# Two fused transformer-like layers on one core: another order of TensorE's work in the attention loop, the routing fold moved into its first units, finer waits at GpSimd's gathers, and a shorter computation of the tile table

## The reference

```python
# x: 32 sequences x 64 tokens x 512 (2048 tokens)
# layer 0: h = x @ cond_w[subject];  x += (silu(h @ gate * gs) * (h @ up * us)) @ down * down_s
# layer 1, attention: 8 query heads, 4 key/value heads of 64; a paged cache of 16-token blocks
q, k = rope(rms(x Wq)), rope(rms(x Wk)); v = x Wv
k_blocks, v_blocks get the new tokens' rows; keys and values are read back through the block table
scores = q k^T / 16, allowed: key position in (pos - 256, pos]
y = softmax(scores) v @ Wo
# layer 1, mixture: logits = clip(y @ gate_w.T); top 2 of 8 experts; rw = softmax(top_w)
# each expert adds a sparse matrix (4096 entries) to W:
# x += y @ W.T + sum_k rw_k * sparse[top_k](y)
```

## Time and profile before

| | us |
|---|---|
| three timed runs | 984.15, 997.46, 1004.24 (median 997.46) |
| the profiled execution | 991.06 |
| its span, first to last instruction | 989.5 |
| TensorE busy | 888.9 (90% of the span) |
| VectorE busy | 651.2 (66%) |
| ScalarE busy | 382.9 (39%) |
| GpSimd busy | 431.0 (44%) |
| mean granted TensorE clock | 0.937 of full |

### The profile page before, as it was taken

How to read it: one execution, slowest core, us unless ns; L and a number is a source line. 1 busy time by engine, 2 the same in 40 slices (tenths; PEclk the granted TensorE clock), 3 DMA queues, 4 the chain that set the end, 5 groups by cost and what they waited for, 6 DMA issues and landing times.

```text
span 989.5 us, 15012 instructions
## 1 busy us (share of the span) xinstructions
PE 888.9 (90%) x4085; PEld 637.7 (64%) x4085; DVE 651.2 (66%) x1875; ACT 382.9 (39%) x869; POOL 431.0 (44%) x492
## 2 busy tenths in 40 slices
PE   5699998999899999967898999998999985999994
PEld 5688656874687478525566666665656654888773
DVE  5654589867886799495657767777766762444332
ACT  2522232224222332464545556766655530111110
POOL 3302334444344300005434665556565523666773
PEclk8599998999999999995879999999999996999998
DMA  8645454023302310544223344434333204743772
GB/s 230 239 127 197 159 198 138 1 49 81 92 1 46 120 43 1 173 147 118 77 60 93 76 115 104 113 104 128 102 97 90 61 23 130 223 148 87 126 114 31
DMA packets 66360, 105.44 MB, mean 107 GB/s; under 512 B 29811, under 2 KB 31107, under 8 KB 66158
## 3 DMA queue, kind: packets, MB, share of 16 engines
q0 software_dynamic: 30368, 50.69, 20.2%
q1 hardware_dynamic: 34974, 52.14, 17.0%
q10 hardware_dynamic: 944, 1.74, 0.6%
HBM read 91.63 MB, written 37.49 MB: 130 GB/s over the span
## 4 chain that ended last, share of the span: by engine, by line
PE 50%; DVE 16%; DMA 14%; issue 8%; POOL 4%; ACT 4%; SPq 2%; DVEq 0%; POOLq 0%; ACTq 0%
PE bank L799 14%; PE bank L810 8%; PE bank L948 6%; PE bank L933 6%; DMA mine<-list_dram 6%; PE bank L922 4%; PE bank L913 3%; PE bank L832 3%; DMA q_t<-q_dram 3%; POOL out_dram L2044 2%; DMA up_raw<-in_up_t 2%; DMA out_dram<-z_sb,mine 2%; PE bank L892 2%; PE bank L942 2%; DVE raw L1612 2%
## 5 line engine op out<-in xcount | busy, mean ns | idle before, releaser
L549 POOL DMA_INDIRECT kv_t<-kv_dram,own_new x64 | 68.9, 1076 | 179.3 <-DMA kv_dram<-kv_out 111.6
L933 PE MATMUL bank<-pT,kv_t 128*128 128x256 f32 (+1 forms) x384 | 115.6, 422 | 0.0
L832 PE MATMUL bank<-wqkv,x1T 128*128 128x512 f32 x256 | 112.1, 593 | 1.4 <-ACT x1T L1098 1.4
L1680 DVE CUSTOM_DVE_ANT_0 prob<-bank,mask 128x320 f32<-128x320 f32 x128 | 57.8, 487 | 71.8 <-PE bank L913 65.4
L1187 ACT ACTIVATE pT<-bank 128x384 f32<-128x384 f32 x128 | 55.8, 486 | 118.9 <-PE bank L922 118.3
L534 POOL DMA_INDIRECT kv_t<-in_kv_cache,own_cache x64 | 67.0, 1047 | 57.8 <-PE bank L933 39.3
L1086 ACT ACTIVATE silu<-bank,gs 128x512 f32<-128x512 f32 x44 | 30.2, 690 | 158.2 <-PE bank L799 158.2
L832 PEld LDWEIGHTS bank<-wqkv,x1T 128*128 128x128 f32 x256 | 47.7, 190 | 57.5 <-issue 57.5
L933 PEld LDWEIGHTS bank<-pT,kv_t 128*128 128x128 f32 (+1 forms) x384 | 64.1, 193 | 30.1 <-issue 22.2
L799 PE MATMUL bank<-hT_hi,gate_w 128*128 128x512 f32 x176 | 72.7, 413 | 6.9 <-DVE hdn L1523 5.3
L1256 ACT ACTIVATE zT_hi<-bank 128x512 fp32r<-128x512 f32 x44 | 26.3, 598 | 131.9 <-PE bank L1024 131.9
(11 more groups left out here) (313 smaller groups left out, 2005.2 us busy)
## 6 DMA issues: line engine op xcount, KB each, us to landing
table_dram<-wexp POOLq DMA_DIRECT2D x16, 512.0 KB, 2.9
xr<-in_x SPq DMA_DIRECT2D x4, 1024.0 KB, 6.8
yx_dram<-x SPq DMA_DIRECT2D x16, 256.0 KB, 2.3
q_dram<-q_out SPq DMA_DIRECT2D x16, 256.0 KB, 2.1
kv_dram<-kv_out SPq DMA_DIRECT2D x16, 256.0 KB, 2.3
early_stage<-table_dram SPq DMA_DIRECT2D x8, 512.0 KB, 8.1
q_t<-q_dram SPq DMA_DIRECT2D x16, 256.0 KB, 3.6
stage<-table_dram SPq DMA_DIRECT2D x16, 256.0 KB, 3.2
```

The source lines that it names most:

```text
L549: pool.indirect_dma_start(kv_t[q % KVB][0:rows, c, :], None, kv_dram, bass.IndirectOffsetOnAxis(own_new[0:rows, at:at + 1], 0), bounds_che ...
L832: mm = pe.matmul(bk(2 * (j % 2) + half), x1T[:, k, j * P:(j + 1) * P], wqkv[:, k, half * T:(half + 1) * T], start=(k == 0), stop=(k == KT ...
L933: mm = pe.matmul(bk(O_BANKS[q % 2])[:, gp * 2 * P:(gp + 1) * 2 * P], kv_t[q % KVB][0:rows, c, v:v + 2 * HD], pT[0:rows, n % 2, c, :, :].re ...
L1680: dve.tensor_tensor_reduce(prob[s % PROBS][:, :], bk(s % 2)[:, 0:KEYS], mask[:, s // 4 % 2, :], MASKED, MASKED, ALU.add, ALU.min, mx[:, s ...
```

## The change

- In the attention loop TensorE does the two `turn_p` of unit `n` first, then `score(n + 2)`, `turn_q`, `turn_k(n + 3)`, and `values(n)` in place of `values(n - 1)`. ScalarE does its two `pT_copy` ahead of the exponentials.
- The turning of `wo` moves into units 0 to 3 (`turn_wo(n)` behind `values(n)`), the fold into unit 4; `wr_ready` is first waited for in unit 5.
- SyncE loads `q` of pair p + 2 between its two table pieces, ahead of `store_y`; the first table pieces are loaded at pair 2.
- GpSimd: cache gathers count on semaphores of their own (`cache_in`, one for each chunk), and each of the two gathers of new rows waits for its chunk alone; `list_entry` comes behind them; the waits for gathers of sequences 0 and 1 and for `wr_ps` go. The cast of the entries goes to VectorE.
- AHEAD is 4, so that two low parts leave the way into the attention and the last in the loop is at unit 54. 14 small memsets and copies of constants are done by VectorE ahead of the loop.
- The end: `project_o` of the last two pairs goes behind the last `logits` and `places`; the totals come with the last `places` from `ab` and `counts`; the last pair writes to a tile of its own (`oT_last`); the tile table gives the list rows (`rows_ready`) ahead of the experts (`tiles_ready`), in fewer steps; the first 22 tiles wait only for the lists of the first choice.

```diff
+                pe.wait_ge(cache_in[c], 16 * max(q + 1, 2))   # gather_new: pool, for each chunk c
@@ TensorE, attention loop
                 for n in range(UNITS):
                     p, at = n // 4, n % 4
+                    turn_p(2 * n)
+                    turn_p(2 * n + 1)
                     if n + 2 < UNITS:
                         score(n + 2)
                     if at == 1 and p + 1 < PAIRS:
+                        if p == 1:
+                            pe.wait_ge(wr_ready, 1)
...
                         turn_q(p + 1)
-                    turn_p(2 * n)
-                    turn_p(2 * n + 1)
...
-                    if n >= 1:
-                        values(n - 1)
+                    values(n)
+                    if n < KT:
+                        turn_wo(n)
+                    elif n == KT:
+                        fold_route()
                     if at == 2 and p >= 1:
                         pe.wait_ge(kT_ready, min(n + 4, UNITS))
...
                         if p + 1 < PAIRS:
                             pe.wait_ge(qT_ready, 2 * p + 4)
-                        project_o(p - 1)
+                            project_o(p - 1)
@@ TensorE, the end
-                values(UNITS - 1)
                 places(final - 1)
                 logits(final)
+                project_o(final - 1)
+                places(final)
+                pe.wait_ge(y_ready, final)
                 project_o(final)
-                places(final)
-                pe.wait_ge(entry_ready, PAIRS)
-                pe.matmul(bk(5)[:, 4 * E:6 * E], ones_sq[:, :], counts...).then_inc(all_ps, 1)
@@ ScalarE, attention loop
+                    pT_copy(2 * n)
+                    pT_copy(2 * n + 1)
                     if n + 1 < UNITS:
                         exponential(2 * n + 2)
                         exponential(2 * n + 3)
...
-                    pT_copy(2 * n)
-                    pT_copy(2 * n + 1)
@@ SyncE, attention loop
+                        if at == 0 and p + 2 < PAIRS:
+                            sp.wait_ge(qT_ps, p + 2)
+                            load_q(p + 2)
                     if p >= 1:
                         store_y(p - 1)
-                    if p + 2 < PAIRS:
-                        sp.wait_ge(qT_ps, p + 2)
-                        load_q(p + 2)
@@ GpSimd, attention loop
                     gather_cache(pool, q)
                     gather_own(pool, q)
+                    gather_new(pool, q)
                     if p >= LISTED_BEHIND:
-                        if b == 0:
-                            round_entry(p - LISTED_BEHIND)
                         list_entry(p - LISTED_BEHIND, b)
-                    pool.wait_ge(kv_gathered[q % KVB], q // KVB * GATHERS + 16 * 3)
-                    pool.sem_inc(taken, 1)
-                    gather_new(pool, q)
```

More of the change, by code:

```diff
@@ L524, in bass_adaln_ffn_kernel @@
         taken = sem("taken")
+        cache_in = [sem(f"cache_in{c}") for c in range(2)]
         kv_gathered = [sem(f"kv_gathered{u}") for u in range(KVB)]
@@ L588, in bass_adaln_ffn_kernel @@
         entry_ready = sem("entry_ready")
-        entry_rounded = sem("entry_rounded")
-        entry_stored = sem("entry_stored")
+        entry_stored = [sem(f"entry_stored{a}") for a in range(2)]
         mask_ready = sem("mask_ready")
@@ L611, in bass_adaln_ffn_kernel @@
         HALVES = 2 * EARLY * EPIECES
-        AHEAD = 6
+        AHEAD = 4
         def low_item(n):
@@ L730, in _ @@
                 load_q(1)
-                sp.wait_ge(wr_ps, 1)
-                for piece in range(STAGES):
-                    load_piece(piece)
                 for p in range(PAIRS):
+                    if p == 2:
+                        sp.wait_ge(wr_ps, 1)
+                        for piece in range(STAGES):
+                            load_piece(piece)
                     for at in (0, 2):
@@ L900, in turn_q, with turn_wo, fold_route @@
                     mm.then_inc(qT_ps, 1)
+                def turn_wo(n):
+                    if n == 0:
+                        pe.wait_ge(wo_loaded, 16)
+                        pe.wait_ge(route_loaded, 16)
+                    elif n == 2:
+                        pe.wait_ge(qT_ready, 4)
+                    else:
+                        pe.wait_ge(woT_ready, n)
+                    for k in range(KT):
+                        mm = pe.transpose(bk(7 - n // 2)[:, k * P:(k + 1) * P], wo[:, k, n * P:(n + 1) * P], ident[:, :])
+                    mm.then_inc(woT_ps, 1)
+                def fold_route():
+                    pe.wait_ge(woT_ready, KT)
+                    for k in range(KT):
+                        for n in range(KT):
+                            mm = pe.matmul(bk(6)[:, k * E:(k + 1) * E], woT[:, n, k * P:(k + 1) * P], route_w[:, n, :], start=(n == 0), stop=(n == KT - 1))
+                    mm.then_inc(wr_ps, 1)
                 def score(n):
@@ L1249, in _ @@
                 route_exp(final)
+                y_copy(final - 1)
                 y_copy(final)
@@ L1759, in low_part @@
                                       experts_hi[EARLY + k][:, :, at].bitcast(F32), ALU.subtract).then_inc(experts_ready, 1)
-                for half in range(4):
+                for half in range(3):
                     early_low(half)
@@ L1814, in _ @@
                 choose(final - 1)
+                dve.wait_ge(pT_ps, 2 * UNITS - 2)
+                dve.memset(seven[:, :], 0.0)
                 weigh(final - 1)
@@ L1829, in tstep @@
                     dve.wait_ge(tile_step, t.n)
-                tstep(*[dve.memset(octal[:, j:j + 1], float(E ** j)) for j in range(PACK)], dve.memset(seven[:, :], 0.0))
-                dve.wait_ge(all_ps, 1)
                 tstep(dve.tensor_scalar(total_i[:, :, :], bk(5)[:, 4 * E:6 * E].rearrange("p (a e) -> p a e", e=E), float(P - 1), None, ALU.add))
```

165 lines of the change are left out of this document (84 added, 81 removed).

## The result

The changed kernel takes 1029.1 us (median of 4 executions, 1018.56 to 1041.59); the kernel before, on the same chip, 993.1. The ratio is 1.036, interval 1.020 to 1.051: 3.6% slower. The forecast of 994 and its range up to 1009 were wrong.

The account below looks back on a forecast made before the run. VectorE was taken to bound 12.37 us of each pair, TensorE 8.51. Terms 7.2 - 0.7 - 2.9 + 2 - 5.2 = +0.4 on 991.06 gave 991; forecast 994, since that execution lay below the median; range 976 to 1009.

Parts of the forecast that it names:

- stretch A: Loop, from the score at `at == 3` to that at `at == 2`: set by VectorE, to stay at 12.37 us.
- Stretch B: Rest of each pair, TensorE's: new 0.6 us hole ahead of places, 8.51 to 9.11 us, +7.2 over 12 pairs.
- The clock, four to five falls, +2: Attention loop: TensorE's clock falls four to five times instead of three, each costing 1.7 us; +2 us.
- the clock falls and sticks: Rival, loop: TensorE stays at half clock for several units; three such falls, +20 us, 1014 us; chance 0.12.
- The queries' load, -0.7: Loop: queries load some 10 us earlier and the wait goes, mostly hidden in VectorE's time; -0.7 us together.
- The way in, -2.9: Start of attention: first score 2.5 us earlier, fold and turning moved inside, a gather's wait gone; -2.9 us.
- the -6.0 for the slow stretch: Way in: without the wait for sequence 4's gather, the half-clock stretch behind it goes too; -6.0 us.
- The gathers: GpSimd's finer gather waits: no cost or gain in the loop, where no TensorE wait is for a gather.
- The end, -5.2: From the last values to SyncE's first list load: shorter path to the table, load about 5.2 us earlier.
- The step on what gates the load: End: the last list entry gates SyncE's first list load, at about -5.2 us; list rows alone -6.0.
- ScalarE becomes late: Rival, stretch A: exponentials 0.3 us late per unit, each pair 0.9 longer; +11 us, 1005 us; chance 0.10.
- The clock stays up: Rival: no clock falls in loop or at fold, smaller hole ahead of places; about 12 us less, 982; chance 0.24.

Follow-up runs that it names:

- a_project_first: Changed kernel with the projection of the pair before put ahead of the wait for the keys' low part, places and logits at unit 2: 1026.3 us, ratio 1.032.
- b_narrow: Kernel before plus four unused 8-column matmuls between logits and projection of each pair: 1019.1 us, ratio 1.026.
- b_queries_early: Kernel before with SyncE loading each pair's queries right behind the first low part, ahead of the store of y: 1010.5 us, ratio 1.012.
- a_order_back_fill: Changed kernel with the old TensorE and ScalarE loop order, plus one unused 512-column matmul ahead of the score at unit 2 of each pair: 1003.9 us, ratio 0.998.

## Why the prediction was wrong

- **"The work per pair is the same", stretch A stays at 12.37: failed.** The instructions are the same, their durations from start to start aren't. Values, turn_p and turn_k cost 0.42 more a unit by their new neighbours, so three units went from 9.87 to 11.13. TensorE became late for VectorE's first mask of `at == 0`, in a stretch that I had given to VectorE alone, and the rest of VectorE's row follows it. A is 12.96. I had the four steps from one order and carried them to another.
- **Stretch B +0.60, from 8.51 to 9.11: right.** 9.05. Places started 3.43 behind the score, as forecast, waiting for the keys' low part; the hole is 0.46 and not 0.60, because TensorE's own steps ahead of it got longer. The pair took 21.4 instead of 22.0 when a_project_first took it out.
- **The clock, four to five falls, +2: failed, and the largest term.** 13 falls, 12 of them in the 12 pairs, where they cost some 21 us more than before. The rival "the clock falls and sticks" had the condition right (the row of values, hole, places, logits meets the drop in more than one pair of four) and its 1014 still counted three falls; I gave it 0.12. I took falls as rare hits of a drifting pair, and didn't ask whether a pair with a fall becomes long enough to meet the next one. b_narrow shows that more narrow work can bring a fall in every pair; that the length repeats the falls is argued from the spacings.
- **The queries' load, -0.7: wrong in sign.** The wait went, and its going costs 1.2% in b_queries_early: there the idle time is one hole ahead of the score, and the clock falls behind it. In the changed kernel the idle time stands in two holes of 0.54 and 0.56, so this price can't be carried over to it as it is.
- **The way in, -2.9: failed in the changed kernel (+5.4 at pair 2).** The first score came 1.1 earlier, not 2.5, since the keys of sequence 0 were there at 456.18, not at 454.9. The gather of sequence 4 is no longer waited for, as forecast. From the first score to the first projection it then took 49.6 us instead of 42.8 (458.31 to 507.86, 459.41 to 502.21), where I had about none more. The largest term that failed is the -6.0 for the slow stretch: the clock was at half until 477 instead of 469, and again behind the fold from 494.0 to 500.5, in all 25.6 us of this part against 22.3. The gathers, which I had at nothing in the loop, stand at 0.999 against 0.995 in the runs with the filler, and the intervals overlap.
- **The end, -5.2: 4.2 where no fall disturbed it, 1.0 in the changed kernel.** The list rows take 3.2 from the totals (853.28 to 856.50, forecast 3.1). The step on what gates the load failed: not the last entry's store but SyncE's last store of `y`, and with it the last projection, which I had called off the path. It costs little here, since the rows were ready only 0.4 before that store was done. 0.9 is given back at the first fetch.
- **ScalarE becomes late: not so.** In the pairs up to 790 us TensorE never waited for its pT copies, behind that once for 1.8 us. "The clock stays up", with 0.24, was the wrong way round.

The sum that would have held: 5.4 at pair 2; 33.5 in the 12 pairs, of which 6.5 are B and 7.1 are A by the one pair at full clock, and some 20 the clock; 1.1 behind them, 1.0 gained up to the first list load and 2.1 lost from there on (40.0 in all).

## What to carry to other kernels

The price of a matmul depended on its neighbour here; when an order changes, take each step from a place in the trace where the same two stand together. On a loop whose clock falls now and then, count narrow work and holes per pair. Ask too whether a pair with a fall gets the length that puts the next narrow row at the same distance. A wait removed can cost more than it took, if it leaves one larger hole (b_queries_early). A wide unused matmul in a hole that another engine sets anyway can then be cheaper than the hole (a_order_back_fill).

## What the runs showed of the hardware

- The clock falls without any long pause (largest hole 1.6 us): 0.89 us more of narrow matmuls in a pair made a fall in every pair (clock .92 over 12 pairs), 0.94 us of one wide matmul in the same place six in all (.94).
- Falls repeated with the loop: mostly 23.5 to 24.0 us apart in three kernels whose pair with one fall takes 23.3 to 24.0. The cause isn't shown.
- A pass of 64 rows beside 64-row work was cheaper than beside 128-row work: values step 1.42 against 1.64 to 1.69, turn_k before a 64-row chunk 0.42 against 0.52.
- The same kernel's executions differ by 2% in one series, and their time follows the mean clock (985.20 at .949, 1005.08 at .926). One of ten executions of a_order_back_fill took 1502.68 us at a mean clock of .554; no cause was found.
